# Two reorderings in a fused two-layer attention kernel: POOL's layer-norm shift before the early attention step, and base_values after the first score maxima on DVE

## The reference

```
x = x + L0_xattn(layernorm(x), ctx)            # 16 heads of 8, rotary embedding
x = x + L0_ffn(layernorm(x))                   # ternary weights, relu, 128 -> 512 -> 128
x = x + L1_xattn(layernorm(x), ctx, mask)      # 16 query heads, 4 key/value heads, causal and mask,
                                               # layernorm of the output, then Wo
x = x + L1_ffn(layernorm(x))                   # 8 experts, the best one for each token
```

## Time and profile before

| | us |
|---|---|
| median of 3 runs | 599.77 (598.32 to 601.37) |
| the profiled execution | 599.77 |
| its span, first to last instruction | 598.0 |
| PE busy | 500.4 (84% of the span) |
| DVE busy | 397.4 (66%) |
| POOL busy | 382.4 (64%) |
| ACT busy | 357.7 (60%) |
| PE's mean granted clock | 0.96 of full speed |

### The profile page before, as it was taken

How to read it: one execution, slowest core, us unless ns; L and a number is a source line. 1 busy time by engine, 2 the same in 40 slices (tenths; PEclk the granted TensorE clock), 3 DMA queues, 4 the chain that set the end, 5 groups by cost and what they waited for, 6 DMA issues and landing times.

```text
span 598.0 us, 20120 instructions
## 1 busy us (share of the span) xinstructions
PE 500.4 (84%) x6238; PEld 365.6 (61%) x6239; DVE 397.4 (66%) x1205; ACT 357.7 (60%) x872; POOL 382.4 (64%) x790
## 2 busy tenths in 40 slices
PE   3568988999888799988999999989987814999992
PEld 2346666666665599875555555555654414999992
DVE  7657777777897456536578898898886661444440
ACT  3246776777766455653567767777764633666661
POOL 7877666676762356676466788888884560555553
PEclk9989999999999899998899999999998965999997
DMA  6634343434331940023344544455443124333330
GB/s 164 178 90 121 85 126 79 119 91 117 94 90 40 300 105 1 2 66 95 88 107 108 127 118 105 116 135 137 118 99 80 41 83 102 88 95 92 93 88 27
DMA packets 102161, 59.92 MB, mean 100 GB/s; under 512 B 20338, under 2 KB 98178, under 8 KB 102098
## 3 DMA queue, kind: packets, MB, share of 16 engines
q1 hardware_dynamic: 98738, 51.79, 34.7%
q0 software_dynamic: 2784, 6.82, 3.4%
q10 hardware_dynamic: 576, 0.53, 0.3%
HBM read 19.90 MB, written 8.81 MB: 48 GB/s over the span
## 4 chain that ended last, share of the span: by engine, by line
PE 39%; SPq 15%; issue 11%; DVE 11%; POOL 9%; DMA 9%; ACT 3%; ACTq 0%; DVEq 0%; POOLq 0%
SPq L395 8%; DMA stack<-pieces 5%; PE scoreT L772 5%; DVE negmax L1410 5%; PE bank L782 5%; PE bank L668 4%; PE score L612 3%; PE bank L846 2%; PE bank L555 2%; SPq L456 2%; DMA stack<-negpT 2%; PE bank L527 2%; POOL expert_rows L1232 2%; PE scoreT L834 2%; PE bank L683 2%
## 5 line engine op out<-in xcount | busy, mean ns | idle before, releaser
L1410 DVE TENSOR_REDUCE negmax<-score 128x8 f32<-128x1024 f32 x128 | 156.2, 1220 | 35.3 <-PE score L612 28.3
L955 ACT ACTIVATE P<-scoreT 128x1024 f32<-128x1024 f32 x128 | 131.0, 1024 | 42.0 <-PE scoreT L632 24.9
L668 PE MATMUL bank<-P,Vc 128*32 128x128 f32 x2048 | 82.7, 279 | 1.3 <-DVE product L1518 1.2
L612 PE MATMUL score<-stack 64*128 64x128 bf16 x1024 | 62.7, 222 | 20.8 <-DMA stack<-pieces 11.5
L1314 POOL DMA_INDIRECT out<-by x39 | 40.0, 1025 | 39.1 <-issue 13.8
L612 PEld LDWEIGHTS score<-stack 64*128 64x128 bf16 x1024 | 33.8, 95 | 47.9 <-issue 23.0
L668 PEld LDWEIGHTS bank<-P,Vc 128*32 128x32 f32 x2048 | 48.4, 109 | 15.3 <-issue 2.7
L961 ACT COPY outs<-bank 128x256 f32<-128x256 f32 x64 | 23.7, 370 | 51.2 <-PE bank L668 51.1
L1175 POOL TENSOR_TENSOR pieces<-full,pieces 128x256 bf16<-128x256 f32 x64 | 42.9, 670 | 13.9 <-ACT pieces L936 13.9
L1178 POOL TENSOR_TENSOR pieces<-rest,pieces 128x256 bf16<-128x256 f32 x64 | 44.3, 692 | 5.0
L1186 POOL TENSOR_TENSOR negp<-negmax,blank 128x16 bf16<-128x16 f32 x64 | 17.0, 266 | 42.3 <-DVE negmax L1410 40.8
(11 more groups left out here) (211 smaller groups left out, 1256.9 us busy)
## 6 DMA issues: line engine op xcount, KB each, us to landing
stack<-pieces SPq DMA_DIRECT2D x192, 128.0 KB, 2.7
ctxT<-in_ctxT SPq DMA_DIRECT2D x32, 128.0 KB, 2.6
XB<-expert_rows SPq DMA_DIRECT2D x39, 66.0 KB
XA<-expert_rows SPq DMA_DIRECT2D x39, 64.0 KB
XR<-in_x SPq DMA_DIRECT2D x4, 512.0 KB, 4.5
stack<-blank SPq DMA_DIRECT2D x32, 64.0 KB, 2.0
stack<-negpT SPq DMA_DIRECT2D x64, 32.0 KB, 1.9
M<-in_M SPq DMA_DIRECT2D x1, 2048.0 KB, 9.9
```

The lines of the kernel that those rows point to most:

```text
L612: mm = nc.tensor.matmul(SCORE[:, r, i * 128:(i + 1) * 128], Qs[pb][rows, h, tb * S:(tb + 1) * S], Ks[pb][rows, kv, tb * S:(tb + 1) * S], s ...
L668: mm = nc.tensor.matmul(PVOUT[VCOL * i:VCOL * (i + 1), half * 128:(half + 1) * 128], Vc[:, k % BODY, at:at + VCOL], P32[:, c, i * 128:(i + ...
L955: nc.scalar.activation(P32[:, half * 2:half * 2 + 2, :], SCORET[:], ACT.Exp, scale=SCALE).then_inc(sem("exp_done"), 1)
L1410: nc.vector.tensor_reduce(negmax[:, k % 2, :, half * HQ:(half + 1) * HQ], SCORE[:].rearrange("p r (h k) -> p r h k", h=HQ), AX.X, ALU.max, ...
```

## The change

Two calls are moved, one on POOL and one on DVE; nothing is added or removed, and PE, ACT and SP keep their programs.

```diff
             def ffn_step(p, b):
                 ffn_rstd(p + 4, b)
                 ffn_bias(p + 2)
-                run_early(early, p)
                 if b == 1:
                     pool.wait_ge(sem("x1_stats"), 4 * p + 4)
                     x_shift("shifted1", slice(2 * p - 2, 2 * p + 2), 4, p // 2)
                     x_deviation(slice(2 * p - 2, 2 * p + 2), p // 2)
+                run_early(early, p)
...
                 def step(t, j):
                     if L and j % 2 == 1:
                         values(j + 3)
-                        base_values(j + 5)
                     add_out(t - 3, j - 3)
                     maxima(t + 2, 0, j + 2)
+                    if L and j % 2 == 1:
+                        base_values(j + 5)
```

## The result

The changed kernel takes 608.15 us (median of four runs, 606.05 to 611.41), the kernel before 600.09 us on the same chip (598.32 to 601.37). The ratio is 1.0125, with a 95% interval of 1.009 to 1.016: some 7.5 us slower. The forecast was 605.5 us with a range of 601.7 to 609.0. Executions of one kernel differ by 1 to 2% here (the changed one 604.31 to 611.90 us in 37), so what follows takes total times from medians, and from a single trace only where in it time is lost. The profiled execution of the changed kernel took 607.01 us, its span is 605.2 us against 598.0.

What follows compares the result with a forecast made beforehand. No one engine bounds the whole: PE and DVE alternate at the hand-over, a POOL-PE-DVE loop in the attention steps. Span 598.0 + 2.6 + 3.1 = 603.7 us, 1.8 more for the execution: 605.5 us, range 601.7 to 609.0.

Steps and rivals of the forecast that it cites:

- Slower through two waits: Likeliest case: both the hand-over and the attention steps are paid, 605.5 us; chance 0.57.
- the first two rivals: Only the hand-over is paid, 602.4 us, chance 0.10; or only the attention steps, 602.9 us, chance 0.11.
- the fourth: Rival: not slower; base_values falls into DVE's idle time and the hand-over is hidden; 598.7 us, chance 0.09.
- The hand-over, +2.6 us: From first FFN to layer-1 attention, pair 15: POOL's shift delays the split and PE's L695, L555 and scores; 2.6 us.
- The clock: PE's half-rate stretch from 280 us: 1.7 us less or more; the middle was taken, adding nothing.
- The third rival: PE's pause lengthens its low-clock stretch by one or two times 3.4 us: 607.2 to 608.9 us; chance 0.13.
- The sign that the forecast named for the clock: After the hand-over: the low-clock stretch ending much sooner or later than 3 us behind 288 would refute the middle.
- The steps, +3.1 us: Odd attention steps, 327 to 403 us: L555 waits for base_values, delaying DVE's second reduction; seven steps total 3.1 us.
- part 2: DVE's half of the change: base_values put behind the first reduction L1410; forecast to cost 3.1 us, bounds 0 and 4.3.
- the first rival's slack: Attention steps: DVE's own queue, not PE, sets the pair, so L555's delay costs nothing; 602.4 us, chance 0.10.
- the odd step at 427 us: Attention step where L555 would be 0.46 us later, but a wait behind it hides that: nothing.
- The cover at pairs 11 and 13: POOL's later cuts there cost nothing, since ACT or SP takes them up later anyway; 0.5 us without that cover.

Runs made afterwards that it cites:

- e1: Only POOL's shift moved ahead of the early attention step, DVE as before, against the kernel before: 602.38 us, ratio 1.0103.
- e2: Only DVE's base_values moved behind the first reduction, POOL as before, against the kernel before: 601.61 us, ratio 1.0087.
- e10: Changed kernel plus seven useless matmuls on PE ahead of the transpose of batch 0's maxima and two ahead of step 0's scores: 599.08 us, ratio 1.0051 to before.
- e11: The changed kernel measured and traced again, nothing further changed, on a second chip: 606.22 us, ratio 1.0147 to the kernel before.
- e4: Changed kernel plus fourteen useless matmuls on PE ahead of the transpose of batch 0's maxima: 600.55 us, ratio 1.0082 to the kernel before.
- e5: POOL's shift moved ahead at pairs 11 and 13 but not at 15, DVE as before, against the kernel before: 597.09 us, ratio 1.0011.
- e3a: Kernel before with PE's key projection L555 moved behind the second half of the scores in odd steps: 597.79 us, ratio 0.9993.
- e6: Kernel before with POOL's add_bias and indirect scatter of the even step put behind the next split of the maxima: 599.08 us, ratio 1.0036.
- e9: Kernel before plus useless matmuls in PE's hand-over pauses, one ahead of L555 and two ahead of step 0's scores: 597.88 us, ratio 1.0024.
- e8: Kernel before with key and query projections and base logits behind the second half of the scores, odd and even steps: 606.99 us, ratio 1.0164.

## Why the prediction was right, and where its sizes were off

**Slower through two waits: right.** e1 and e2 each cost time by themselves, so the first two rivals (only one of the places is paid) fall, and with them the fourth. That the two costs add fits the times; the intervals don't prove it.

**The hand-over, +2.6 us: right for the order.** POOL's L1134 was forecast near 277.0 and stands at 277.66 (DVE's statistics came 0.6 us later in this execution), L695 near 280.1 and stands at 280.95, and the wait for POOL of over 3 us is 3.72. At full clock the order costs 2.8 us (e10). The scores forecast at 281.0 and 283.2 came at 282.12 and 284.83, later by the statistics' 0.6 us and by the clock.

**The clock, "I take the middle, since the low stretch is there already": this is the term that failed.** The trace has it in two pieces. At once, L555 and the scores behind the pause run at 1.2 GHz: the first jump is 3.7 us in the changed kernel, 3.7 in e1 and e11, and 2.8 in e10, so 0.9 us is the clock's. Later, where the low stretch lasts to 297 us, another 1.8 us comes on top (e1: 3.86 to 5.69; e11: 5.00 to 6.84). The hand-over costs 3.7 us where 2.6 was summed, and 5.5 to 5.6 us in executions with the long stretch. The third rival had the mechanism: it lengthened the low stretch by one or two times 3.4 us, at 1.7 to 3.4 us of time. Measured are 3.3 us longer for 0.9 us (10.2 against 6.9) and 10.1 us longer for 2.7 us. It was given 0.13 as another case; it was a part of the likeliest one, and 608.15 us lies in its band of 607.2 to 608.9. The sign that the forecast named for the clock, a stretch that ends much sooner or later than 3 us behind 288, didn't show in the first execution of the changed kernel (3.4 us behind it) and did in e1 and e11 (8 to 9 us behind it). The reason given for the middle was weak: before, the pauses ahead of 280 us are 0.53, 0.37 and 1.05 us, and one of 3.7 us is another thing.

For the rule that the forecast set beside it (the Trainium skill, "TensorE: Matmul & The Clock Gate", "HAM oscillation": the price is the throttled time times one half), e10 has the number: 6.9 us of low stretch cost 2.6 us, not 3.4. The 10.2 us of the changed kernel come to 3.5 us by the same table (2.6 and 0.9), not 5.1, and the 17 us to 5.3, not 8.5. So the rule is too high here; these traces fit with a path that PE doesn't hold in all of the stretch, which I did not show.

**The steps, +3.1 us: right in kind, too large in size, with 4.0 in the trace of the changed kernel.** L555 waits as forecast (0.46 us on average for its weight load, 0.26 for the product in the step shown), DVE's wait for the second scores at 399.82 is 0.78 where 0.8 was said. The three pairs that took 37.9 us before take 38.9 (L555 from 359.01 to 397.87), where 39.3 was forecast: not every late second reduction makes the next first one as late. The second halves jump by 0.3 to 0.5 us in each odd step from batch 13 to 21 and a part comes back at the next first half. From the second half of batch 8 to the first of batch 22, the seven steps that were summed to 3.1 us cost 2.1 us in e10, at full clock; e2, e4 and e11 have 1.8, 2.0 and 1.4 there, if 1.4 us is taken off each for the low stretch near 398 us, and the changed kernel 2.1 without the jump that comes next (e1, without part 2, drifts by 0.8 over the same steps, so tenths are not to be trusted). So this term was a third or more too large: a part of the first rival's slack is there. That the trace of the changed kernel comes to 4.0 is not what was forecast but two things beside it. One is a jump of 1.26 us at batch 10, second half: there PE's transposed scores wait 0.80 us for the transfer of the transposed maxima, with the clock at 1.00.

```profile
337.78 0.28 PE L591 MATMUL scoreT<-negI,mask 64*128 64x256 bf16 x2 [0.80 <-DMA stack<-negpT]
```

It shows in none of e1, e2, e10 and e11, so I take it as an accident of that execution. The other is the odd step at 427 us, which was costed at nothing "with a wait of the same kind behind it": its 0.6 us is paid (batch 25, 7.25 to 7.89, and 8.00 after it; in e10 1.25 to 1.76 and 1.73, behind a fall from 2.17 to 1.25 that the changed kernel has little of). For the step at 314 us the same argument held: 4.06, 4.83, and back to 4.08.

**The cover at pairs 11 and 13: right** (e5).

**The sum.** 2.6 + 3.1 was 5.7; 3.7 + 4.0 is what the trace has, 7.7. The median of 608.15 us is inside the range, and the mechanisms are those forecast, but the sum is near by some luck: the steps were put 1.0 us too high or more, the clock behind the hand-over 0.9 to 2.7 us too low, and both traces of the changed kernel pay another 1.3 to 1.4 us, one by the jump and one (e11) by a low stretch near 399 us, that no term had.

**What stays open.** How long the clock stays down is not settled by the kernel: 10.2 us and 17 us for the same program. Why it fell near 398 us in e2, e4 and e11 and not in e10 or in the first execution of the changed kernel is open too; what the first three share is that PE had been idle for 0.9 to 1.2 us of a stretch of 2 us ahead, but the kernel before has 0.98 us of idling there (388 to 390 us), the first execution of the changed kernel 1.24 us (396 to 398 us), and in both the clock stays up. And the parts alone cost more than both together by their medians; the intervals allow that this is noise.

## What to carry to other kernels

Moving a short operation costs nothing by itself; look at the engine that waits for it. Here 0.08 us out of DVE's way stood against 0.5 us in the way of PE, and on POOL a wait for DVE and 2 us of work were put ahead of the only thing that PE could go on with. Where a change makes TensorE stand still for some microseconds, put the slower clock behind the pause into the likeliest case, not beside it. And before taking a wait out, look at what would be late next: three edits to the kernel before that took away a wait or a slow stretch (e3a, e6, e9) gained nothing, and a fourth (e8) lost 9.8 us.

## What the runs showed of the hardware

- The length of PE's low stretch behind a pause of 3.7 us varied between executions: 10.2 us in one of the changed kernel, 17 us in the other, 17.1 us in e1, with PE busy for most of that time (5.53 to 6.69 of 8 us from 280 to 288 us, 4.00 of 4.00 from 288 to 292 in all three). The clock came back while the work went on as before.
- Before, a low stretch of 6.9 us began without any single pause of more than 1.05 us at the hand-over.
- Filling PE's pauses there with useless products kept the clock at 2.4 GHz from 274 to 304 us in the changed kernel (e4, e10), but in the kernel before it only put the low stretch off by 11 us (e9).
- A low stretch of 3.4 us in the middle of the attention (e2: 2 us times 0.24, 0.50 and 0.11, twice) cost 1.4 us, by its growth beside e10's over the same steps.
- The clock fell in the middle of the attention (304 to 456 us) in four of the six traces in which L555 waits for base_values there, and in none of the eight others.
